# A two-layer spectral kernel: the mixing stage's weight loads all on SyncE's queue, its sums stored by ScalarE

## The reference, cut to what matters

```
multiplier = symmetric_padding(complex(weight_real, weight_imag), (128, 128), (128, 128))
x_ft   = symmetric_padding(rfftshift(rfft2(gn(x))), ...)
out_ft = einsum('bixy,ioxy->boxy', x_ft, multiplier)    # 32 channels in, 32 out
out    = x + irfft2(irfftshift(out_ft), s=(128, 128))
```

## Time and profile before

| | |
|---|---|
| median of 3 runs | 1069.66 us (1069.3 to 1073.97) |
| profiled execution | 1070.72 us, span 1069.1 us |
| busy share of the span | PE 75%, DVE 63%, ACT 38%, POOL 34% |
| mixing stage | first product at 693.18 us, last at 981.21 us |
| weights | 128 transfers of 520 KB |
| TensorE's granted clock | 0.901 of full on average |

### The profile page before, as it was taken

How to read it: one execution, slowest core, us unless ns; L and a number is a source line. 1 busy time by engine, 2 the same in 40 slices (tenths; PEclk the granted TensorE clock), 3 DMA queues, 4 the chain that set the end, 5 groups by cost and what they waited for, 6 DMA issues and landing times. The chain is left out here.

```text
span 1069.1 us, 36892 instructions
## 1 busy us (share of the span) xinstructions
PE 799.1 (75%) x16113; PEld 589.4 (55%) x16113; DVE 678.4 (63%) x1459; ACT 403.4 (38%) x915; POOL 368.1 (34%) x262
## 2 busy tenths in 40 slices
PE   0499296989999846999905999366677777777797
PEld 0365142322222216888705999366666667666686
DVE  4897388778888784566568999635544444553132
ACT  0298252122323263555533666323333333331121
POOL 0022373889999801111100000324434444442000
PEclk9999598899999967999957999788888888988899
DMA  9566633465555230454122665769999999997687
GB/s 364 112 188 160 137 73 104 148 255 190 182 176 183 97 79 22 155 129 114 42 67 79 175 182 158 161 153 272 262 262 266 265 266 266 269 268 164 182 243 216
DMA packets 270336, 189.43 MB, mean 177 GB/s; under 512 B 29396, under 2 KB 259509, under 8 KB 269045
## 3 DMA queue, kind: packets, MB, share of 16 engines
q1 hardware_dynamic: 190003, 131.56, 45.9%
q10 hardware_dynamic: 75138, 44.14, 17.1%
q0 software_dynamic: 5120, 12.75, 4.2%
HBM read 154.50 MB, written 33.07 MB: 175 GB/s over the span
## 5 line engine op out<-in xcount | busy, mean ns | idle before, releaser
L2035 PE MATMUL po<-pa,room 128*32 128x16 f32 x8320 | 148.0, 220 | 85.7 <-DMA room<-_L_conv_weight_imag_dram 59.0
L2035 PEld LDWEIGHTS po<-pa,room 128*32 128x32 f32 x8320 | 145.2, 163 | 94.0 <-issue 78.9
L981 POOL TENSOR_TENSOR q<-lead 128x1536 f32<-128x1536 f32 (+1 forms) x51 | 170.2, 3365 | 28.0 <-POOLq L650 13.8
L1080 DVE TENSOR_TENSOR q<-pw,lead 128x1536 f32<-128x1536 f32 (+1 forms) x85 | 140.6, 1704 | 15.7 <-PE acc L1026 10.2
L2176 DVE TENSOR_TENSOR osl<-po,neg 128x128 f32<-128x128 f32 x64 | 18.4, 287 | 151.2 <-ACT neg L2109 151.2
L1026 PE MATMUL acc<-q,pt 128*32 128x384 f32 (+1 forms) x1088 | 102.4, 486 | 14.3 <-DVE q L1080 14.3
L1988 POOL DMA_DIRECT2D os_<-osl x64 | 45.3, 713 | 184.0 <-DVE osl L2187 176.1
L1978 POOL COPY cols<-y 128x512 f32<-128x512 f32 x32 | 38.3, 1197 | 145.2 <-POOLq L1744 139.8
L2109 ACT ACTIVATE neg<-po 128x272 f32<-128x272 f32 x32 | 12.7, 397 | 199.7 <-issue 184.7
L2022 PE MATMUL px<-wbat,cols 128*32 128x130 f32 x2176 | 76.3, 293 | 3.0 <-DVE wbat L2147 3.0
L1026 PEld LDWEIGHTS acc<-q,pt 128*32 128x32 f32 x1088 | 27.5, 109 | 87.1 <-issue 57.2
(11 more groups left out here) (335 smaller groups left out, 1582.5 us busy)
## 6 DMA issues: line engine op xcount, KB each, us to landing
room<-_L_conv_weight_real_dram ACTq DMA_DIRECT2D x32, 520.0 KB, 9.8
room<-_L_conv_weight_imag_dram ACTq DMA_DIRECT2D x32, 520.0 KB, 12.6
room<-_L_conv_weight_real_dram SPq DMA_DIRECT2D x32, 520.0 KB, 7.1
room<-_L_conv_weight_imag_dram SPq DMA_DIRECT2D x32, 520.0 KB, 10.4
lead<-xns SPq DMA_DIRECT2D x64, 192.0 KB, 3.1
lead<-wv SPq DMA_DIRECT2D x16, 576.0 KB, 5.9
yall<-in_x_dram SPq DMA_DIRECT2D x4, 2048.0 KB, 14.5
xd<-in_x_dram SPq DMA_DIRECT2D x16, 512.0 KB, 4.2
```

The costliest lines, as they stand in the source:

```text
L981: nc.gpsimd.tensor_tensor(q2[:, t % 2, :, :, 0:m], bc(weights(blk, n), 2, NB), spectra(blk), ALU.mult).then_inc(s_qp, 1)
L1080: V.tensor_tensor(q1[:, t % 2, :, :, 0:m], bc(pw[t % 4][:, 0:3 * m].rearrange("p (r m) -> p r m", r=3), 2, NB), spectra(blk), ALU.mult).th ...
L2035: e = nc.tensor.matmul(po[u][32 * g:32 * g + 32, 512 * q + 16 * m:512 * q + 16 * m + 16], wsl[u][:, :, q * KWF + KWF - 1 - kw], xsl[u][:, ...
```

## The change

In the mixing stage SyncE issues all four loads of a chunk, `p` = 0 and then `p` = 1, on its queue. ScalarE issues no loads; it issues the chunk's two stores, after the copies for the next spectrum. GpSimd issues no transfers and no longer waits for the stores' end (SyncE still does). Sizes, buffers and arithmetic stay.

```diff
@@ sync
                 for c_ in range(NCHK):
                     wait(sp, s_ms, c_ - 1)
-                    load_weights(sp, 0, c_)
+                    for p in range(2):
+                        load_weights(sp, p, c_)
@@ gpsimd
-                def store(c_):
-                    u = c_ % 2
-                    pool.wait_ge(s_oc, c_ + 3)
-                    n = NT * 4 * NB * 32
-                    for e in range(2):
-                        pool.dma_start(bass.AP(os_.tensor, ...), osl[:, u, e].rearrange("p q b m -> p q (b m)")).then_inc(s_os[u], 16)
...
                 for c_ in range(NCHK):
                     columns(c_ + 2)
-                    store(c_)
-                for q in s_os:
-                    pool.wait_ge(q, 32 * NCHK // 2)
@@ scalar
-                load_weights(act, 1, 0)
-                load_weights(act, 1, 1)
...
+                def store_pairs(c_):
+                    u = c_ % 2
+                    act.wait_ge(s_oc, c_ + 3)
+                    n = NT * 4 * NB * 32
+                    for e in range(2):
+                        act.dma_start(bass.AP(os_.tensor, ...), osl[:, u, e].rearrange("p q b m -> p q (b m)")).then_inc(s_os[u], 16)
...
                 for c_ in range(NCHK):
                     act.wait_ge(s_ms, c_ + 1)
-                    if c_ + 2 < NCHK:
-                        load_weights(act, 1, c_ + 2)
                     act.wait_ge(s_oc, c_ + 1)
                     act.activation(neg[...], mixed(c_)[...], ACT.Copy).then_inc(s_nc, 1)
                     if c_ + 2 < NCHK:
                         rows(c_ + 2)
+                    store_pairs(c_)
```

More of the change, by code:

```diff
@@ L1981, in columns @@
                         nc.gpsimd.memset(cols[:, u, 0, 0, 0:1], 0.0).then_inc(s_col, 1)
-                def store(c_):
-                    u = c_ % 2
-                    pool.wait_ge(s_oc, c_ + 3)
-                    n = NT * 4 * NB * 32
-                    for e in range(2):
-                        pool.dma_start(bass.AP(os_.tensor, (NP * e + SL * c_) * n, [[NB * 32, 128], [n, SL], [1, NB * 32]]),
-                                       osl[:, u, e].rearrange("p q b m -> p q (b m)")).then_inc(s_os[u], 16)
                 columns(0)
@@ L2101, in rows @@
                     m.then_inc(s_xa, 1)
+                def store_pairs(c_):
[3 more added lines that the diff above has]
+                    for e in range(2):
+                        act.dma_start(bass.AP(os_.tensor, (NP * e + SL * c_) * n, [[NB * 32, 128], [n, SL], [1, NB * 32]]),
+                                      osl[:, u, e].rearrange("p q b m -> p q (b m)")).then_inc(s_os[u], 16)
                 rows(0)
```

## The result

| | before | after |
|---|---|---|
| median | 1069.48 us (1068.18 to 1073.97, 4 runs) | 1153.64 us (1152.7 to 1155.83, 4 runs) |
| ratio | | 1.0775, 95% interval 1.0752 to 1.0798 |
| span of the profiled execution | 1069.1 us | 1151.6 us |
| last product of the stage starts | 981.21 us | 1065.78 us |
| a chunk of the stage | 9.03 us | 11.75 us |

The changed kernel is 7.75% slower. The loss lies whole in the mixing stage: its last product starts 84.6 us later, and the rest of the span is 85.8 us instead of 87.9.

A forecast was written before the change was run, and what follows sets the result against it. Transfers were taken to bound the mixing stage; 12.07 us of loads plus 0.3 of stores, 12.4 us over 32 chunks, plus 0.7, put its last product 95.2 us later: 1165 us, range 1105 to 1215.

The forecast's parts named there:

- step 1: Mixing-stage loads: one queue writes one block of 32 partitions at a time, 176.5 GB/s, 12.07 us a chunk.
- The sum: Mixing stage: first data at 678.9 us, 32 chunks of 12.4 us, 0.7 us; last product at 1076.4, total 1165 us.
- the rival of the skewed engines: Mixing-stage loads: DMA engines drift apart by around half a chunk, 235 GB/s, 10.2 us a chunk, total 1095 us; 12%.
- step 4: Stores issued by ScalarE share the DMA engines with the weights: 0.3 us a chunk, 1.5 if wholly in series.
- step 2: SyncE's load queue never runs dry, 7.5 us of work left at each issue; the period is the transfer time.
- step 5: End of the mixing stage: last lower transfers cost 0.7 us; last stores from ScalarE within 0.5 us, taken as nothing.
- One deep queue at full rate, faster or the same: Mixing-stage loads: one queue gives 295 GB/s, 8.1 us a chunk, 1041 us, 5%; with dips kept 1070 us, 5%.
- ScalarE held by its stores: Mixing stage: stores wait behind SyncE's blocked loads, ScalarE needs 14.2 us a chunk, total 1223 us; 8%.

The follow-up runs named there:

- e7: Changed kernel with a chunk's four loads reordered on the one queue: lower real, upper real, lower imaginary, upper imaginary; 1144.33 us, ratio 1.0687.
- e5: Kernel before, but SyncE loads real parts and ScalarE imaginary parts, each lower half first, so both are meant to write the same half; 1138.21 us, ratio 1.0621.
- e3: Changed kernel with each load writing every fourth partition instead of a block of 32, so output values differ; 1029.08 us, ratio 0.9603.
- e10: Kernel before, two load queues, with each load writing every fourth partition, so output values differ; 1032.81 us, ratio 0.964.
- e1: Kernel before with all loads on SyncE's queue, stores still issued by GpSimd; 1159.85 us, ratio 1.0823.
- e11: Kernel before with ScalarE loading its imaginary part first, each queue keeping its half; 1072.98 us, ratio 1.0.
- e4: Changed kernel with each load writing all 128 partitions, 8 packets each, so output values differ; 1030.60 us, ratio 0.9625.
- e6: Kernel before, but SyncE loads real parts, lower half first, and ScalarE imaginary parts, upper half first; 1108.92 us, ratio 1.0357.

## Why the prediction was right, step by step
- *The rate (step 1).* Right, and the mechanism was the forecast one. Forecast 176.5 GB/s; measured 177 inside a half (see e7), which makes 12.0 us of a chunk. The stage's mean is 181 because of the changes of half. Each gives back 0.15 us, 0.3 us a chunk. The sum had put this at nothing; the rival of the skewed engines had the mechanism, at a far larger size.
- *The stores (step 4).* Forecast 0.3 us a chunk, with 1.5 as the other bound; measured 0.04. In the 2.5 us in which they move, q1 gets 164 GB/s (0.41 MB), but it makes up for it: in the us from 856 to 857, with only the stores' last packets beside it, it moves 0.25 MB. Over the quarter of a chunk's packets that this touches it is 3.05 us against 3.01 at 177 GB/s.

```profile
q1 hardware_dynamic: 476, 0.25, 117.2%
```

- *Both together* made the chunk 12.4 where 11.75 was measured: 0.65 x 32 = 21 us too much. These are the two mis-sized terms, 0.26 us for the stores and 0.3 for the changes of half; the rest is the rate's 0.05 and rounding. The two points that follow took 9 us of it back.
- *No gap (step 2).* Right in the steady stage, wrong at its start. From 704 to 708 us the queue ran dry, and behind chunk 1's product it thinned out again:

```profile
702.00:704.00 2.00, 0.34 (x21) 0.34 (x24) 0.00 (x0) 0.00 (x0) 0.00 (x0) 0.50 1.10 155
704.00:706.00 2.00, 1.94 (x119) 1.83 (x114) 0.00 (x0) 0.00 (x0) 0.00 (x0) 0.50 0.14 26
706.00:708.00 2.00, 0.61 (x14) 0.58 (x17) 0.00 (x0) 0.33 (x1) 0.00 (x0) 0.50 0.00 0
720.00:722.00 2.00, 2.00 (x91) 2.00 (x95) 0.23 (x2) 0.40 (x1) 0.00 (x0) 0.50 0.69 106
722.00:724.00 2.00, 2.00 (x52) 1.83 (x44) 1.14 (x10) 0.00 (x0) 0.00 (x0) 0.71 0.51 103
```

The chain of the same place, after and then before, shows what PE did:

```profile
697.90 5.76 issue
...
714.30 5.60 issue
```

```profile
695.50 3.22 issue
...
709.38 3.66 issue
```

PE stood still inside its first pass through the product's loop for 5.76 and 5.60 us, in waits for nothing that the profile shows, where the kernel before had 3.22 and 3.66. Chunk 0's product ended at 707.64 instead of 702.7 us: 2.4 us of this because it began later, 2.5 because the first stall was longer. The loads of chunk 2 came after the queue had emptied. Against 181 GB/s the first gap, with the start into the empty queue, cost 5.4 us and the second 1.8, some 7 us together. The forecast had used chunk 0 and 1 as if they were steady ones, with a product of 4.6 us. The trace of before already had 9.5 us there, from 693.18 to 702.70. What PE waited for I can't show. The queue named q8 instruction has one packet of 16 KB in each of these stalls, 0.7 and 1.2 us into them before and 2.7 and 2.9 after. That fits a loading of PE's instructions held up by weights under way, but no run tests it.
- *The start.* SyncE's first load came at 678.90, 2.07 us later than in the profile of before, from ahead of the stage. No run shows why.
- *The sum, redone:* first data at 681 us, 32 x 11.75 = 376, 0.7 for the small packets, 7 for the gaps: 1064.7, measured 1065.78. So 1165 came near 1153.64 partly by luck: the chunk was forecast 21 us too long in all, and the late start and the gaps took 9 back.
- *The end (step 5).* Nothing forecast. From the last product's start to the last store's landing it was 981.21 to 990.74 us before; after:

```profile
1065.78 4.44 PE po L2026 x256
...
1072.53 1.95 DMA os_<-osl
```

that is 1074.48 - 1065.78 = 8.7 against 9.5 us: 0.8 us gained.
- *The rivals.* One deep queue at full rate, faster or the same: refuted by 204 GB/s; in e5 even two queues did no better while they wrote one half. Only with transfers that reach all partitions did the number of queues not count (e3, e10). The rule behind it, from the Trainium skill, SBUF — State Buffer, section "Can I just issue two DMAs to hit both halves?", gives two such transfers only 6% over one. By that rule, these runs disagree: the kernel before moves 31% more than e1 (236 against 180 GB/s), and e11 (234) does the same. The same section of the Trainium skill names one transfer over all 128 partitions as the only way to all ports. By that rule, e4 agrees in that such a transfer reaches the full rate (273 against 181 GB/s), but it isn't the only way: from 684 to 692 us of the earlier trace rows two queues with a half each moved 295. ScalarE held by its stores: refuted, 0.9 us for both issues; what came late was the stores' packets, by some five us, within the slack. Skewed engines: right in kind, at each change of half, but 0.3 us a chunk in place of the 2.2 that the rival had.

## What to carry to other kernels
Ask of each queue not how many bytes it has but which partitions it writes at one time: transfers into 32 neighbouring partitions belong on two queues, one kept to partitions 0 to 63 and the other to 64 to 127, and neither should change its half. Where a layout allows it, let each transfer span all partitions; the queue then hardly matters. Here it was worth 4% in kernels whose products no longer find their weights; a layout in which they do wasn't built. When two queues carry a double-buffered load, give the small transfers to the queue that empties first, behind the loads (2% here, against half a per cent on the queue that empties last).

## What the runs showed of the hardware that I had not expected
- Two queues with fixed halves are 31% faster than one, but two that change halves within a chunk (e6) lose about half of that: 205 GB/s against 234 with fixed halves (e11). Two in the same half at a time move 172 GB/s of weights (e5), though they write different blocks of 32 partitions.
- One queue gains for a moment when its next load changes the half: up to 215 GB/s instead of 177, 0.15 us a change (the changed kernel and e7).
- A partition step of 4 in the destination gives one queue 271 GB/s instead of 181, with everything else alike (e3), as much as 128 partitions do (e4, 273).
- Stores issued by ScalarE at 848.8 and 849.2 us moved from 854.3 us on, while SyncE's issues of loads were held. The issues of both engines may pass through one place in order; no run tests that.
- The stores, read from all partitions, go almost beside the weights: 335 GB/s in the us from 855 to 856 of the changed kernel, where weights alone make 177, and 0.04 us a chunk in the end:

```profile
855.00:856.00 1.00, 1.00 (x76) 1.00 (x71) 0.00 (x0) 0.00 (x0) 0.00 (x0) 0.50 1.14 335
```
